# Where the last state update stands, the order of two ScalarE jobs, and later group statistics

## Time and profile before

| what | us |
|---|---|
| median of three runs | 3776.11 |
| the profiled execution, as timed | 3791.09 |
| its span | 3789.3 |
| PE busy | 3493.5 (92%) |
| DVE busy | 2754.8 (73%) |
| ACT busy | 2654.8 (70%) |
| POOL busy | 1603.1 (42%) |
| mean granted clock of PE | 0.986 |

### The profile page before, as it was taken

One profiled execution on the slowest core, in us unless ns is written; L12 is line 12 of the kernel. 1 busy time (PEld: TensorE's weight loads), 2 busy tenths in 40 slices (PEclk: granted clock), 3 DMA queues, 4 the chain that ended last, 5 costly groups with the idle time before them and its releaser, 6 DMA issues.

```text
span 3789.3 us, 84370 instructions
## 1 busy us (share of the span) xinstructions
PE 3493.5 (92%) x27988; PEld 2845.5 (75%) x27988; DVE 2754.8 (73%) x6715; ACT 2654.8 (70%) x7096; POOL 1603.1 (42%) x1557
## 2 busy tenths in 40 slices
PE   1669999999999999999999999999999999999898
PEld 0238787787878778787877878787787878778787
DVE  7776876767777676777767777776767867575746
ACT  2347776777777777777767777776776777677675
POOL 5542452625445262544626254462625536150402
PEclk9889999999999999999999999999999999999999
DMA  6662534536353453635446264444626344360302
GB/s 221 197 204 68 173 116 140 171 97 192 113 169 114 142 174 92 192 118 159 124 130 187 85 192 124 148 131 123 197 75 191 119 143 119 103 190 1 112 12 79
DMA packets 559907, 515.10 MB, mean 136 GB/s; under 512 B 97601, under 2 KB 491969, under 8 KB 559553
## 3 DMA queue, kind: packets, MB, share of 16 engines
q1 hardware_dynamic: 555200, 508.99, 44.5%
q10 hardware_dynamic: 4352, 1.57, 0.2%
HBM read 351.06 MB, written 134.22 MB: 128 GB/s over the span
## 4 chain that ended last, share of the span: by engine, by line
PE 79%; DVE 9%; ACT 7%; issue 3%; DMA 1%; SPq 1%; POOL 0%; ACTq 0%; DVEq 0%; POOLq 0%
PE F L1546 16%; PE SM L1529 15%; PE VAB L1546 8%; PE PP L1637 8%; PE F L1585 6%; PE T L1557 5%; PE VAB L1585 5%; PE VAB L1615 5%; PE T L1606 3%; PE F L1548 3%; PE T L1625 2%; ACT K L1310 2%; PE VAB L1548 1%; ACT K L1316 1%; DVE K L1002 1%
## 5 line engine op out<-in xcount | busy, mean ns | idle before, releaser
L1546 PE MATMUL F<-WQ,XHL 128*128 128x256 f16 x6144 | 813.6, 273 | 16.0 <-ACT V L1347 16.0
L661 POOL TENSOR_TENSOR XR<-XR,V 128x512 f32<-128x512 f32 x256 | 325.6, 1272 | 902.6 <-DVE XR L1057 902.6
L636 POOL TENSOR_TENSOR SL<-PL,SL 128x1122 f16<-128x1122 f32 x112 | 259.6, 2318 | 978.4 <-DVE SL L970 978.4
L1316 ACT ACTIVATE K<-K,SCAL 128x256 f32<-128x256 f32 x1024 | 514.0, 509 | 222.2 <-DVE K L1002 221.3
L1546 PEld LDWEIGHTS F<-WQ,XHL 128*128 128x128 f16 (+1 forms) x6144 | 600.3, 98 | 90.0 <-issue 19.9
L1529 PE MATMUL SM<-SL,BD 128*128 128x512 f16 x2688 | 634.9, 385 | 0.0
L1310 ACT ACTIVATE K<-F,SCAL 128x256 f32<-128x256 f32 x1024 | 474.0, 469 | 194.1 <-DVE F L996 192.0
L1002 DVE TENSOR_TENSOR K<-K,F 128x512 f32<-128x512 f32 x512 | 350.4, 684 | 204.6 <-PE T L1557 113.8
L996 DVE TENSOR_TENSOR F<-F,FL 128x512 f32<-128x512 f32 x512 | 354.0, 691 | 178.8 <-PE F L1548 173.7
L1529 PEld LDWEIGHTS SM<-SL,BD 128*128 128x128 f16 x2688 | 260.9, 97 | 284.2
L1637 PE MATMUL PP<-XR,WP 128*128 128x256 f16 x3072 | 380.4, 274 | 45.3 <-DVE XR L1075 44.7
(11 more groups left out here) (202 smaller groups left out, 6856.5 us busy)
## 6 DMA issues: line engine op xcount, KB each, us to landing
XR<-xr SPq DMA_DIRECT2D x132, 512.0 KB, 5.1
U<-x SPq DMA_DIRECT2D x256, 256.0 KB, 3.4
XR<-x SPq DMA_DIRECT2D x256, 256.0 KB, 4.2
out<-XR SPq DMA_DIRECT2D x256, 256.0 KB, 3.4
PL<-xp SPq DMA_DIRECT2D x112, 561.0 KB, 3.8
RX<-xr SPq DMA_DIRECT2D x118, 512.0 KB, 3.8
x<-RX SPq DMA_DIRECT2D x448, 128.0 KB, 2.8
BD<-RX SPq DMA_DIRECT2D x240, 96.0 KB, 2.2
```

The source lines that it names most:

```text
L661: g_.tensor_tensor(o, o, fm, ALU.add).then_inc(o_rdy, 2)
L1316: a.activation(K2[:, p, t * C:(t + 1) * C], K3[:, p, t * C:(t + 1) * C], ACT.Square, scale=inv_a, accum_out=S6[:, 2 * p + t:2 * p + t + 1] ...
L1546: t_.matmul(o, XHL[:, xa, h, at], WQ[:, wa, h, c0:c0 + C], start=(k == 0), stop=False)
```

## The change

Five edits, all in the order of work; no instruction of arithmetic is added or removed.

1. PE does only the last but one update of the state before the depthwise convolution. The last one and the closing matmuls (`last_state`) come behind channel 1. On DVE `low_v` of the last pair goes ahead of `ratio` and `scale_k`, since the convolution waits for it.
2. The five small matmuls of the norms come two channels later (19, 21, 25, 28, 30 for 17, 19, 23, 26, 28), and ACT's root behind channel 23 for 21.
3. PE's wait for all 32 `fm_rdy` behind the convolution goes. The first query pair waits for channel 28 (the last in bank F0), the second for all 32.
4. In ACT's `step_q`, `high_out` stands ahead of `attn_input`.

```diff
 # vector, batch
+                low_v(b, NU - 1, 1)
                 ratio(n, 1, S2, S6)
                 scale_k(n, 1)
-                low_v(b, NU - 1, 1)
                 if s3:
                     pixel_stats(b + 3, 0)
                 state(b)
 # scalar, depthwise
-                    if ahead >= 1 and c == 21:
+                    if ahead >= 1 and c == 23:
                         root(b + 4)
 # scalar, step_q
+                if live(p - 3):
+                    high_out(b, u - 2 + p, 1 - p)
                 if nxt:
                     attn_input(b + 1, u - 3, p)
-                if live(p - 3):
-                    high_out(b, u - 2 + p, 1 - p)
 # tensor
+            def last_state(b):
+                accumulate_state(b, NU - 1, 1)
+                for h in range(HALVES):
+                    fin = t_.matmul(T[h][:, 0:P + 2], ONES[0:32, :], NOT[:, :], start=False, stop=True)
+                fin.then_inc(state_full, 1)
...
                     ins.then_inc(dw_full, 1)
-                    if ahead >= 1 and c == 17:
+                    if c == 1:
+                        last_state(b)
+                    if ahead >= 1 and c == 19:
                         group_mean(b + 4)
-                    if ahead >= 1 and c == 19:
+                    if ahead >= 1 and c == 21:
                         group_spread(b + 4)
-                    if ahead >= 3 and c == 23:
+                    if ahead >= 3 and c == 25:
                         patch_mean(b + 3)
-                    if ahead >= 3 and c == 26:
+                    if ahead >= 3 and c == 28:
                         hidden(b + 3)
-                    if ahead >= 3 and c == 28:
+                    if ahead >= 3 and c == 30:
                         heads(b + 3)
...
                     pe.wait_ge(f_cube, b * 2 * PAIRS + PAIRS + 2 * u + p + 1)
+                    if u == 0:
+
+                        pe.wait_ge(fm_rdy, HD * b + (HD - 3 if p == 0 else HD) + FM_CR)
+                        carry(pe)
                     project(b, u, p, F, 0)
...
-                for p in range(2):
-                    accumulate_state(b, NU - 1, p)
-                for h in range(HALVES):
-                    fin = t_.matmul(T[h][:, 0:P + 2], ONES[0:32, :], NOT[:, :], start=False, stop=True)
-                fin.then_inc(state_full, 1)
+                accumulate_state(b, NU - 1, 0)
                 pe.wait_ge(v_lo, PAIRS * (b + 1) + VLO_CR)
                 pe.wait_ge(f_cube, b * 2 * PAIRS + PAIRS + CUBE_CR)
                 carry(pe)
                 pe.wait_ge(tp_rdy, CHUNKS)
                 depthwise(b, ahead)
-                pe.wait_ge(fm_rdy, HD * (b + 1) + FM_CR)
-                carry(pe)
                 pe.wait_ge(state_rdy, 4 * HPH * (b + 1))
```

## The result

| kernel | median, us | range of runs | ratio to before (95%) |
|---|---|---|---|
| before | 3776.61 | 3775.22 to 3788.28 | |
| changed | 3736.39 | 3734.60 to 3737.74 | 0.9886 (0.9866 to 0.9907) |
| changed, in a second comparison | 3734.26 | 3732.78 to 3739.91 | 0.9881 (0.9867 to 0.9895) |

The change, the four numbered edits above, takes 40.2 us off, or 44.0 in the second comparison (3778.29 before). The forecast was 29.1 us off, to 3747.0, with a range that ended at 3737. The direction was right. The gain was larger than forecast, and 3736.39 lies just outside the range.

The account below looks back on a forecast made before the run. PE, busy 92% of the span, was taken to bound the kernel, so only its idle time could be won. 18.7 + 2.9 + 7.5 = 29.1 us off the median 3776.11 gave 3747.0, range 3737 to 3768.

Parts of the forecast that it names:

- State update behind two channels: End of stage 1: last state update behind two convolution channels loses its 0.90 us wait; 1.17 us an image, 18.7 us.
- What comes later through it: Norms' small matmuls reached 0.76 us later, DVE's state copy 0.4 us later; `patch_mean` wait of 0.24 us stays; no cost.
- Last channel: PE's 1.01 us wait before the queries goes; nothing gained in images 0 to 12, 2.9 us from the others.
- High half first: Last steps of an image: exchange on ACT cuts the projection's wait by 0.70, stall costs 0.20; 7.5 us in all.
- Port: Image 14: ports shared by DVE and POOL, dead heat of product and subtraction; -8 to +5 us, taken as 0.
- Clock: PE's granted clock falls to 0.50 behind waits at stage 1's end; taken as 0, range -8 to +20 us.
- rival B: Wait moved to the transposes of q brings a clock fall in each of 13 images; 3766.5 us, chance 0.12.
- Rival C: Fewer clock falls before the convolution, and more of the last channel's 16.0 us won; 3739 us, chance 0.12.
- Rivals A: Exchange on ACT brings nothing, as the 0.20 us stall returns in more steps; 3754.5 us, chance 0.12.
- D: Slower: DVE's statistics become stage 2's chain, PE waits before `group_mean` 13 times; 3782.6 us, chance 0.04.

## Why the prediction missed, point by point

- **State update behind two channels: right.** Forecast 1.17 us an image; the timeline shows 1.17, and an undisturbed image is 1.13 us shorter with this edit (222.02 to 220.89).
- **What comes later through it: right.** The wait in front of `patch_mean` stayed at 0.24 us. Without edit 2 a wait in front of `group_mean` would have come, 1.41 us on average in 13 images.
- **Last channel: right.** Nothing in images 0 to 12, 3.2 us in the last three (forecast 2.9). That squash binds there is shown by taking 1.3 us out of it.
- **High half first: size right, in part by luck.** Two small errors cancel. Forecast 0.70 - 0.20 = 0.50 us; undisturbed images give 0.52 (220.89 to 220.37). The stall costs 0.05 and not 0.20, and 0.13 us are lost elsewhere, which I have not traced.
- **Port: the term that I took as 0** was mis-sized: it is 12 x 0.22 = 2.6 us, inside the -8 to +5 that I gave. The exchange alone brings it.
- **Clock: the step that failed.** "I take 0, and keep -8 and +20 us." The terms of order, as measured, are 16 x 1.13 + 15 x 0.52 + 3.2 + 2.6 = 31.7 us. The rest of the 40 to 44 us is 8 to 12 us. The granted clock of the timed runs gives the same size: 0.9910 and 0.9915 for the changed kernel against 0.9884 to 0.9888 in the runs of before, 9 to 11 us by the estimate above. The profiles show 12 and 8 half-clock stretches behind 310 us in the kernel before and 3 and 0 in the changed one, at 1 to 1.8 us each, an estimate from the images above. That falls cost time at waits of this kind is shown by filling one wait (0.9963 to 0.9930). One experiment stands against an exact account: with the waits of before filled, the clock rose to 0.9909 and only 2.8 us were won, where the estimate, with the cost of the filling in it, has 6.5. Why either of these two edits alone lowers the clock stays open.
- The clock paragraph looked only at the falls behind the waits at the state. Four of the 12 stretches in the profile of before start behind the projection's long wait (500, 2726 and 3395 us behind 2.12 us, 3589 behind 2.33), which the exchange shortens to 1.42 and 1.72 us; they were in the trace before the forecast.
- What also misled me was that I set the clock's gain against a loss of 20 us from the new wait of 1.2 us at the transposes (rival B). No profile has a fall there in images 0 to 12 of the changed kernel, although the wait is 1.37 us. Rival C had the right sign, but of its two causes only the clock was true, and I gave it 0.12. Rivals A and D did not happen.

## What to carry to other kernels

Price a wait of the engine that bounds the kernel by two things: its length, and whether the clock falls behind it. In this kernel two places with waits of 1 to 2 us, far apart, could each bring a fall, so easing one showed less than its worth and easing both more than the sum. Put the mean granted clock of the runs beside their times before you explain a difference of some 0.3%, and do not count falls in a single profile. Before a wait is moved, look for what its engine's neighbour does next: here the wait for the last channel only changed places until a table load was taken from ScalarE. When work is put behind other work, move the small chained steps with it; leaving them two channels earlier would have cost some 20 us.

## What the runs showed of the hardware that was not expected

- Useless matmuls in a wait of 2.12 us made a kernel faster, 0.9963 to 0.9930, since TensorE's granted clock no longer fell to 0.50 behind it.
- The wait of 1.44 us at the state stands in every image of the changed kernel, and that of 1.37 us at the transposes in 13; no fall followed them in images 0 to 12. A wait of 2.12 us brought one in six of these images (state edit alone), one of 2.17 us in nine of thirteen; that of 1.42 us at the projection brought none there.
- Single executions of the kernel before differ by up to 16 us within one comparison (3775.71 to 3791.28), those of the exchange alone by 23 us (3762.11 to 3785.22), in step with the granted clock (0.990 to 0.984), those of the changed kernel by 3 and 7 us (3734.60 to 3737.74, 3732.78 to 3739.91).
- A small VectorE product takes 0.16 or 0.83 us, by whether it starts 0.02 us before GpSimd's subtraction or 0.34 us after it.
